# Gathered rows of a product-key layer: weights for two groups at once, two running sums, a ring of 24 rows

## The reference

```python
q = (hidden_states @ w_queries.T).reshape(b, t, 2, h, n)
sim = jnp.einsum('btphn,hkpn->pbthk', q, keys)
sx, ix = jax.lax.top_k(sim[0], k)
sy, iy = jax.lax.top_k(sim[1], k)
...
scores, pos = jax.lax.top_k(all_scores, k)
indices = jnp.take_along_axis(all_idx, pos, axis=-1)
de = down_embed[indices]
ue = up_embed[indices]
ew = jnp.einsum('btd,bthkd->bthk', hidden_states, de)
ew = jax.nn.silu(ew) * jax.nn.softmax(scores, axis=-1)
experts_states = jnp.einsum('bthk,bthkd->btd', ew, ue)
mlp = jax.nn.silu(hidden_states @ w_gate.T) * (hidden_states @ w_up.T) @ w_down.T
return mlp + experts_states
```

## Time and profile before

| | |
|---|---|
| median of 3 runs | 1626.28 us (1619.02 to 1626.79) |
| the profiled execution | 1626.24 us, of which its span is 1624.4 us |
| PE, DVE, ACT, POOL busy | 1293.6, 1102.0, 813.5, 699.8 us |
| mean granted TensorE clock | 0.872 of full speed |
| first gather starts, last gather starts | 308.9 us, 1157.2 us |
| last addition of layer 1 to x starts | 1170.0 us |

### The profile page before, as it was taken

How to read it: one execution, slowest core, us unless ns; L and a number is a source line. 1 busy time by engine, 2 the same in 40 slices (tenths; PEclk the granted TensorE clock), 3 DMA queues, 4 the chain that set the end, 5 groups by cost and what they waited for, 6 DMA issues and landing times.

```text
span 1624.4 us, 18804 instructions
## 1 busy us (share of the span) xinstructions
PE 1293.6 (80%) x5862; PEld 656.6 (40%) x5862; DVE 1102.0 (68%) x2921; ACT 813.5 (50%) x2053; POOL 699.8 (43%) x705
## 2 busy tenths in 40 slices
PE   5989886766678869477658676877889999999998
PEld 3345443243244525333323442443444455444444
DVE  6542417679996786898899998898864234336455
ACT  2454542656757768547558558657735432130110
POOL 2000000388888888854878778888500010010000
PEclk8899998877789979678768787989989999988999
DMA  6000000365575656743656765655310031002000
GB/s 229 23 1 1 10 6 2 63 180 162 164 172 170 187 164 194 183 122 93 179 157 173 223 173 177 182 165 164 110 24 1 1 124 34 1 28 72 1 14 26
DMA packets 59956, 168.67 MB, mean 104 GB/s; under 512 B 15760, under 2 KB 20944, under 8 KB 59216
## 3 DMA queue, kind: packets, MB, share of 16 engines
q0 software_dynamic: 40960, 134.25, 29.9%
q1 hardware_dynamic: 18896, 33.22, 6.3%
HBM read 162.61 MB, written 4.82 MB: 103 GB/s over the span
## 4 chain that ended last, share of the span: by engine, by line
PE 44%; DVE 22%; POOL 18%; issue 10%; ACT 3%; DMA 3%; SPq 0%; DVEq 0%; POOLq 0%; another core or an unknown queue 0%; ACTq 0%
POOL bufR L1851 15%; PE psum L1189 7%; PE psum L1051 6%; PE psum L1063 3%; DVE bufB L1547 3%; DVE bufR L1419 3%; POOL half_sum L1865 2%; PE psum L1108 2%; PE psum L1133 2%; PE psum L854 2%; DMA bufR<-in_table,rowid 2%; PE psum L933 2%; PE psum L986 2%; PE psum L816 2%; DVE x_sb L1437 2%
## 5 line engine op out<-in xcount | busy, mean ns | idle before, releaser
L1851 POOL DMA_INDIRECT bufR<-in_table,rowid x512 | 563.1, 1100 | 240.9 <-issue 124.8
L1214 ACT ACTIVATE bufR<-bufR 128x256 f32<-128x256 f32 x512 | 205.5, 405 | 49.0 <-DVE bufR L1419 37.7
L1419 DVE TENSOR_TENSOR bufR<-bufR 128x1024 f32<-128x1024 f32 x128 | 158.9, 1244 | 48.7 <-DMA bufR<-in_table,rowid 48.0
L854 PE MATMUL psum<-bufB 32*128 32x308 f32 x768 | 95.1, 572 | 93.9 <-DVE bufB L1547 64.7
L1051 PE MATMUL psum<-xtf,wf 128*128 128x512 f32 x320 | 156.3, 634 | 10.3 <-DVE x_sb L1704 7.5
L1547 DVE TENSOR_REDUCE bufB<-psum 128x8 f32<-128x1232 f32 x96 | 137.5, 1436 | 37.1 <-PE psum L854 32.6
L1223 ACT ACTIVATE bufR<-bufR,ew 128x256 f32<-128x256 f32 x128 | 64.0, 504 | 126.0 <-DVE ew L1427 80.9
L1482 DVE TENSOR_TENSOR x_sb<-x_sb,psum 128x256 f32<-128x256 f32 x128 | 50.6, 417 | 106.7 <-PE psum L986 58.6
L1878 POOL TENSOR_TENSOR x_sb<-x_sb,wattn 128x256 f32<-128x256 f32 x16 | 11.1, 730 | 253.9 <-DMA wattn<-in_attn 150.7
L1871 POOL TENSOR_TENSOR x_sb<-x_sb,wattn 128x256 f32<-128x256 f32 x32 | 23.7, 772 | 219.5 <-DMA wattn<-in_attn 161.5
L1811 DVE SCALAR_TENSOR_TENSOR x_sb<-psum,bufR,x_sb 128x256 f32<-128x256 f32 x128 | 61.9, 484 | 75.5 <-PE psum L1189 70.7
(11 more groups left out here) (237 smaller groups left out, 2504.0 us busy)
## 6 DMA issues: line engine op xcount, KB each, us to landing
bufR<-in_table,rowid POOLq DMA_INDIRECT x512
wf<-in_ffn SPq DMA_DIRECT2D x2, 2304.0 KB, 18.6
bufR<-in_ffn SPq DMA_DIRECT2D x1, 2696.5 KB, 17.2
wattn<-in_attn SPq DMA_DIRECT2D x4, 641.0 KB
wf<-in_rope SPq DMA_DIRECT2D x4, 512.0 KB
bufB<-in_ffn SPq DMA_DIRECT2D x1, 2048.0 KB, 8.3
scr_corr<-bufR SPq DMA_DIRECT2D x16, 128.0 KB, 2.3
bufR<-scr_corr SPq DMA_DIRECT2D x4, 512.0 KB, 4.6
```

The lines of the kernel that those rows point to most:

```text
L854: ins = mm(psum[:, at + z, 0:PAR * S], q[r, g, i * P:(i + 1) * P], keysm[r, g, b, :, 0:S], start=True, stop=True)
L1214: own.mark(act(row, row, ACT.Identity, accum_out=dots[:, g % 4, j:j + 1]))
L1419: tt(rows, rows, cast(xg[c % 2][:, i, :].unsqueeze(1), [P, GRP, D]), ALU.mult).then_inc(f1_mu, 1)
L1851: eng.indirect_dma_start(ring[:, s * GRP + j, :], None, io["table"], bass.IndirectOffsetOnAxis(ap=rowid[c % 2][:, at + j:at + j + 1], axis ...
```

## The change

- **Pairs.** The sums of two groups (2h and 2h+1) go to one row of eight. The tanh is taken once for both, behind the odd group, and `weights_of` makes eight weights at once. Weights, additions and the rows' scaling of the even group therefore wait for the odd group's rows.
- **Two sums.** `add_rows` adds rows 0 and 2 to x and row 1 to a tile `second`; only the third instruction waits, for the first. The first group of a tile writes `second` with a multiplication, so it waits for the tile before to be closed (`f1_tile`). `add_half` adds first `second` and then `half_sum` to x.
- **Plan.** `plan()` has the new dependences, new durations for `ew`, `ad` and `ga`, and another set of offsets `PREFER`, so the order of pieces on every engine may differ.

```diff
-RING, GRP = 20, 4
+RING, GRP = 24, 4
...
-             ew=0.41, ad=1.6, ga=0.42, Q=5.6, lg2=5.0, ...
+             ew=0.45, ad=1.5, ga=0.95, Q=5.6, lg2=5.0, ...
...
 PREFER = dict(
-    PE={("Q", 2): -200, ("gu2", 1, 6): -20, ("gu2", 3): 50, ("p1", 1): -160, ...
+    PE={("V3",): 315, ("gu2",): -10, ("gu2", 0): -40, ("p1",): 105, ("s", 2): -40, ...
...
+    POOL={("bo",): 160},
 )
...
-            a = add("ACT", ("th", g), 2.5, m, g >= 4 and ("DVE", ("ew", g - 4)))
-            e = add("DVE", ("ew", g), 0.45, a, g >= 4 and ("ACT", ("sc", g - 4)), g >= 4 and ("DVE", ("ad", g - 4)))
-            s = add("ACT", ("sc", g), 0.5, e)
-            add("DVE", ("ad", g), 1.65, e, outs[i], g and ("DVE", ("ad", g - 1)))
-            p = add("POOL", ("ad", g), 0.8, s, g and ("POOL", ("ad", g - 1)), first and g and ("DVE", ("ga", g - 1)))
+            a = add("ACT", ("th", g), 2.5, m, g >= 4 and ("DVE", ("ew", g // 2 - 2)))
+            if g % 2:
+                e = add("DVE", ("ew", g // 2), 0.45, a, g >= 4 and ("ACT", ("sc", g - 4)), g >= 4 and ("DVE", ("ad", g - 4)))
+                for n in (g - 1, g):
+                    s = add("ACT", ("sc", n), 0.5, e)
+                    add("DVE", ("ad", n), 1.5, e, outs[i], n and ("DVE", ("ad", n - 1)), n % NG == 0 and n and ("DVE", ("ga", n - 1)))
+                    p = add("POOL", ("ad", n), 0.8, s, n and ("POOL", ("ad", n - 1)), n % NG == 0 and n and ("DVE", ("ga", n - 1)))
...
+        def weight(g, j):
+            at = g % 2 * GRP + j
+            return ew[:, g // 2 % 2, at:at + 1]
...
-                own.wait()
-                act(thalf[:, g % 4, :], dots[:, g % 4, :], ACT.Tanh, scale=0.5).then_inc(f1_th, 1)
+                if g % 2:
+                    own.wait()
+                    h = g // 2 % 2
+                    act(thalf[:, h, :], dots[:, h, :], ACT.Tanh, scale=0.5).then_inc(f1_th, 1)
...
-            def weights_of(g):
-                c, s, at = g // UNITS, g % 4, g % UNITS * GRP
-                eng.wait_ge(f1_th, g + 1)
...
+            def weights_of(h):
+                c, z, at = 2 * h // UNITS, h % 2, 2 * h % UNITS * GRP
+                eng.wait_ge(f1_th, h + 1)
+                if h >= 2:
+                    eng.wait_ge(f1_wt, 2 * h - 2)
+                    eng.wait_ge(f1_acc, 2 * h - 2)
+                own.link(stt(ew[:, z, :], dots[:, z, :], 0.5, prob[c % 2][:, at:at + 2 * GRP], ALU.mult, ALU.mult))
+                stt(ew[:, z, :], thalf[:, z, :], 1.0, ew[:, z, :], ALU.add, ALU.mult).then_inc(f1_ew, 1)
...
-                own.link(stt(x, ring[:, at, D:2 * D], ew[:, g % 4, 0:1], x, ALU.mult, ALU.add))
-                own.link(stt(x, ring[:, at + 1, D:2 * D], ew[:, g % 4, 1:2], x, ALU.mult, ALU.add))
-                stt(x, ring[:, at + 2, D:2 * D], ew[:, g % 4, 2:3], x, ALU.mult, ALU.add).then_inc(f1_acc, 1)
+                own.mark(stt(x, rows[0], weight(g, 0), x, ALU.mult, ALU.add))
+                first = own.n
+                if g % NG == 0:
+                    own.mark(ts(second[:, :], rows[1], weight(g, 1), None, ALU.mult))
+                else:
+                    own.mark(stt(second[:, :], rows[1], weight(g, 1), second[:, :], ALU.mult, ALU.add))
+                eng.wait_ge(own_dve, first)
+                stt(x, rows[2], weight(g, 2), x, ALU.mult, ALU.add).then_inc(f1_acc, 1)
...
-                eng.wait_ge(f1_half, g + 1)
-                eng.wait_ge(f1_acc, g + 1)
+                eng.wait_ge(f1_acc, g + 1)
+                own.wait()
+                own.mark(tt(x, x, second[:, :], ALU.add))
+                eng.wait_ge(f1_half, g + 1)
+                own.wait()
                 tt(x, x, half_sum[:, :], ALU.add).then_inc(f1_tile, 1)
...
-    nc = _bacc.Bacc("TRN2", target_bir_lowering=False, num_devices=1)
+    nc = _bacc.Bacc("TRN2", target_bir_lowering=False, num_devices=1, dynamic_dma_scratch_size=4096)
```

More of the change, by code:

```diff
@@ L260, in ffn1 @@
         for g in range(UNITS * c, UNITS * (c + 1)):
-            first, back, last = g % NG == 0, g - SLOTS, g % NG == NG - 1
+            back, last = g - SLOTS, g % NG == NG - 1
             i = g // NG % TI
@@ L265, in ffn1 @@
             m = add("DVE", ("mu", g), 1.3, f, g and ("DVE", ("mu", g - 1)))
[L266 to L270 removed]
+            a = add("ACT", ("th", g), 2.5, m, g >= 4 and ("DVE", ("ew", g // 2 - 2)))
[5 more added lines that the diff above has]
+                    p = add("POOL", ("ad", n), 0.8, s, n and ("POOL", ("ad", n - 1)), n % NG == 0 and n and ("DVE", ("ga", n - 1)))
             if last:
[L272 removed]
+                add("DVE", ("ga", g), 0.95, p, ("DVE", ("ad", g)))
         return out, t
@@ L517, in build @@
         gate2 = sb("gate2", [P, KT * E2])
-        half_sum = sb("half_sum", [P, D])
+        half_sum, second = (sb(s, [P, D]) for s in ("half_sum", "second"))
         prob = [sb(f"prob{z}", [P, P]) for z in range(2)]
@@ L524, in build @@
         work1 = sb("work1", [P, 288])
-        dots, thalf, ew = (sb(s, [P, 4, GRP]) for s in ("dots", "thalf", "ew"))
+        dots, thalf, ew = (sb(s, [P, 2, 2 * GRP]) for s in ("dots", "thalf", "ew"))
         psum = ctx.enter_context(nc.psum_tensor("psum", [P, 8, 512], FP))
@@ L1210, in gathered_sums @@
                 if g >= 4:
-                    eng.wait_ge(f1_ew, g - 3)
+                    eng.wait_ge(f1_ew, g // 2 - 1)
                 for j in range(GRP):
                     row = ring[:, at + j, 0:D]
-                    own.mark(act(row, row, ACT.Identity, accum_out=dots[:, g % 4, j:j + 1]))
-                own.wait()
-                act(thalf[:, g % 4, :], dots[:, g % 4, :], ACT.Tanh, scale=0.5).then_inc(f1_th, 1)
-            def weighted_rows(g):
-                at = GRP * (g % SLOTS)
-                eng.wait_ge(f1_ew, g + 1)
-                for j in (3,):
-                    row = ring[:, at + j, D:2 * D]
-                    ins = act(row, row, ACT.Copy, scale=ew[:, g % 4, j:j + 1])
-                ins.then_inc(f1_wt, 1)
+                    own.mark(act(row, row, ACT.Identity, accum_out=dots[:, g // 2 % 2, g % 2 * GRP + j:g % 2 * GRP + j + 1]))
+                if g % 2:
+                    own.wait()
+                    h = g // 2 % 2
+                    act(thalf[:, h, :], dots[:, h, :], ACT.Tanh, scale=0.5).then_inc(f1_th, 1)
+            def weighted_rows(g):
+                row = ring[:, GRP * (g % SLOTS) + 3, D:2 * D]
+                eng.wait_ge(f1_ew, g // 2 + 1)
+                act(row, row, ACT.Copy, scale=weight(g, 3)).then_inc(f1_wt, 1)
             def deviation(tgt, layer, c):
@@ L1429, in add_rows @@
             def add_rows(g):
                 x, at = x_sb[:, g // NG, :], GRP * (g % SLOTS)
-                eng.wait_ge(f1_ew, g + 1)
+                rows = [ring[:, at + j, D:2 * D] for j in range(3)]
+                eng.wait_ge(f1_ew, g // 2 + 1)
                 if g % NG == 0:
                     eng.wait_ge(f1_x, g // NG + 1)
+                    if g:
+                        eng.wait_ge(f1_tile, g // NG)
                 if g:
                     eng.wait_ge(f1_acc, g)
-                own.link(stt(x, ring[:, at, D:2 * D], ew[:, g % 4, 0:1], x, ALU.mult, ALU.add))
```

19 lines of the change are left out of this document (7 added, 12 removed).

## The result

The changed kernel takes 1628.8 us (median of 20 runs, 1621.88 to 1633.01), the kernel before 1617.45 us (20 runs, 1614.18 to 1628.31). The ratio is 1.0056, 95% interval 1.004 to 1.0071: slower by 9 us (the medians lie 11 us apart), where 23 us less were forecast. The base of the forecast was off as well: the median of the three runs shown before (1626.28) and the profiled execution (1626.24) lie in the upper part of what 20 runs gave, 9 us above their median. So 1603 against 1628.8 shows 26 us of a miss of 32. The profiled execution of the changed kernel took 1629.35 us, its span is 1627.3 us.

A forecast was written before the change was run, and what follows sets the result against it. The prediction took POOL and DVE as near their limit in the gather phase, PE nearly the limit in the tail. Terms of -19, -9 and +5 us gave -23 us, from 1626.24 to 1603 us; range 1573 to 1636.

The forecast's parts named there:

- DVE's sum: DVE's work in the gather phase: additions 29 us and weights 17 us saved, closing tiles 8 us lost, 38 us less.
- The smaller space: Gathers on POOL: the smaller descriptor space was taken to cost nothing.
- the nothing of the sum: Closing a tile on DVE: the wait for `second` was taken as already done, at no cost.
- rival 3: Tile boundaries stall DVE, 2.8 us at each of 16, likewise some pairs' tanh waits: slower, 1657 us; chance 13%.
- From 38 us of DVE to time: Gather phase: DVE's saving becomes -19 us at the gap, -9 us in layer 2's steps, 5 us lost: -23 us.
- The gap, -19 us: POOL's 29.7 us of gaps ahead of chunk 2: the first half's DVE saving shortens them by 19 us.
- The steps of layer 2, -9 us: Second half of the gathers: layer 2's feed-forward steps go ahead, taking 9 us of PE work off the tail.
- The pairs, nothing in the sum: Ring slots and pair waits: the sixth group's slot offsets the even half's wait; 13.3 us of slot waits stay.
- The two sums, 21 us of DVE: DVE's additions to two sums: two links saved for each group, 29 us, less 8 us for closing tiles.
- What I drew from the rule: POOL's gathers and additions beside DVE: with as many two-input DVE instructions, the 85 us of POOL delay stay.
- (1), POOL holds the phase: Gather phase: DVE's time comes free where POOL doesn't wait, the 29.7 us gap stays: 1622 us; chance 16%.

The follow-up runs named there:

- e1: Kernel before with only the descriptor space cut to 4096 bytes a partition; median 1618.9 us.
- e9: Kernel before with small descriptor space and two sums, old order, the kernel of e2 again on another chip; ratio 1.0069 to the kernel before.
- e17: Kernel before with 24 rows, small descriptor space, pairs, one sum, old order, POOL's additions apart, e13 again on another chip; ratio 1.0213.
- e5: Kernel before with 24 rows, small descriptor space, pairs, one sum, old order, POOL's two additions of a pair together; ratio 1.0139.
- e3: Kernel before with small descriptor space and a ring of 24 rows, pieces in the old order; ratio 0.998 to the kernel before.
- e2: Kernel before with small descriptor space and two sums, two tiles `second` in turn, old order; ratio 1.0049 to the kernel before.
- e7: e2 with every addition linked to the one before it; ratio 1.0018 to the kernel before.
- e10: e9 with every addition linked to the one before it, on the same chip; ratio 1.0016 to the kernel before.
- e11: Changed kernel with all three additions of a group linked; ratio 1.0069 to the kernel before, median 1628.95 us.
- e4: All code of the change with pieces in the old order, POOL's two additions of a pair together; ratio 1.0086 to the kernel before.
- e16: Kernel before with 24 rows, small descriptor space, old order, fourth row of odd groups added on DVE instead of ACT and POOL; ratio 1.0324.
- e18: Kernel before with small descriptor space, POOL's copy and addition of the fourth row on 16 of 256 columns; ratio 0.9708, 1570.9 us.
- e15: The kernel of e18 on another chip; ratio 1.0205 to the kernel before, 1663.8 us.
- e8: Kernel before with small descriptor space, old order, row 1 of each group left out of the sum; ratio 0.9893, median 1620.0 us.
- e13: e5 with POOL's additions left where they were, apart; ratio 1.0173 to the kernel before.
- e6: The kernel of e18 on another chip, run earlier; ratio 1.0295 to the kernel before.
- e14: e4 with POOL's additions left where they were, apart; ratio 1.018 to the kernel before.

## Why the prediction was wrong

**What was right.** DVE's sum: 38 us forecast, 41.5 measured (47.1 less in the two stretches of the gathers, 5.1 more behind them). The additions stand as worked out, 0.40 us apart, and the third doesn't wait:

```profile
398.25 0.47 DVE L1451 SCALAR_TENSOR_TENSOR second<-bufR,ew,second 128x256 f32<-128x256 f32 x1
398.64 0.47 DVE L1453 SCALAR_TENSOR_TENSOR x_sb<-bufR,ew,x_sb 128x256 f32<-128x256 f32 x1
399.04 0.15 DVE L1433 SCALAR_TENSOR_TENSOR ew<-dots,prob 128x8 f32<-128x8 f32 x1
```

The gathers start where they did (308.2 us). The smaller space is free as far as e1 shows. POOL's gathers and additions stay as long as they were in the profile before (564.5 and 93.0 us against 563.1 and 90.7). The tile's close waits 18.0 us in 8 of 16 cases: more than the nothing of the sum, less than half of the 45 us that rival 3 had for it.

**The step that failed** is "From 38 us of DVE to time": the terms of -19 us and -9 us, and the pairs' term of nothing. It took POOL's work as a constant with a gap in it, and DVE's time as something that fills the gap. But from 309 to 700 us POOL has hardly an idle stretch over 0.55 us, one in either kernel (0.6 and 0.9 us), so what sets the end there is POOL's own row of instructions. Less work for DVE doesn't shorten that row, and the pairs and the new order put waits into it:

- *The gap, -19 us.* It gave 8, and 6.6 against e1. With 41 us less for DVE the row numbers of chunk 2 came 1 us earlier than in e1, counted from the first gather (432.9 against 434.0), and then the ring held the gather for another 1.2 us. That DVE is busy for 42.7 of the 45 us there is right; that its saved time comes off the gap isn't, and e9, where the wait is as long as in e1, says the same without pairs and new order.
- *The steps of layer 2, -9 us.* None came forward. L1058 (L1051 of the earlier trace rows) by stretch has 120 matmuls in place of 128 up to 1170, and up to its own last addition, which starts at 1174.9, the same 16 steps as before. The part behind the gathers is 465.7 us against 466.3:

```profile
954.00:1170.00 216.00, 68.41 (x120) 26.57 (x120) 0.89 0.57 161
1170.00:1300.00 130.00, 42.08 (x88) 16.85 (x88) 0.96 0.05 11
```

- *The pairs, nothing in the sum* ("the even half has what it had", "I let them stand"). Counted over all groups of the two traces, from a group's first gather to its last addition on DVE lie 24.8 us in the median before and 30.7 after; to POOL's addition 31.8 and 38.5. That is 5.9 and 6.6 us more, where the sixth slot gave 5.6. In the old order pairs and 24 rows cost 34 us (e17), or 23 where POOL's additions stand together (e5, on a chip with stalls). In e17 the even groups live 31.5 us up to DVE's addition and the odd ones 25.7, against 24.9 and 23.4 in e3: the even half doesn't have what it had. The new order pays in another place, with waits for slots, 23.5 us in place of 13.3 (18.8 of them in the gap ahead of chunk 2 that was just counted), and 5.0 of the copy behind the tile's close.
- *The two sums, 21 us of DVE.* They cost 8 to 11 us of time (e2, e9) in the old order, and nothing clear of noise with their links put back (1.0018 and 1.0016 in e7 and e10, both intervals take in 1). The rule of the Trainium skill (SBUF — State Buffer, "SBUF: two separate sides"), that a DVE instruction with two SBUF inputs and a GpSimd instruction that reads SBUF lock each other out for a whole instruction, fits the longer gathers in kind alone. In e1 a gather takes 0.97 us beside neither, 1.00 (142) beside additions alone, 1.24 (101) beside a multiplication alone and 1.315 (84) beside both, so the additions, which have two inputs too, hold it up little by themselves, and the trace agrees with the rule no further than that. What I drew from the rule, that an equal number of instructions gives an equal delay, isn't borne out either: e9 and e10 have the same instructions and differ by 7.9 us of gathers in their profiles and by 7.2 us of time. In the changed kernel's first chunk POOL has no long idle stretch at all, and from its first gather to the next chunk's lie 208.7 us in place of 201.1, with 143.6 us of gathers in place of 137.2. With linked additions (e11) these are 202.5 and 139.2, but chunk 3 is as slow as without links, 210.0 us.

Of the rivals, (1), POOL holds the phase, named the mechanism; its 1622 us, 4 less than its base, still had a gain where 9 us were lost. That 1622 looks near to 1628.8 is luck of the base, and so is that 1628.8 lies in the range of 1573 to 1636 (its lower end is 1574 by its own terms). With the base at 1617.45 the same range would end at 1627.

**What stays open.** The parts don't add up: two sums +8 to +11 and pairs with 24 rows +23 to +34 make more than the +14 of e4, and linking the additions helps without pairs (e10) and not with them (e11). Which part of the new order's remaining 9 us is due to which no run tells. How the loss divides between longer gathers and waits rests on one profile of each kernel. Whether work moved from POOL to DVE (e16) pays on a chip without stalls wasn't measured again.

## What to carry to other kernels

When two engines are near their limit in one phase, add up each one's own timeline, gaps and all, before work taken from the other is turned into time; here 41 us less for DVE gave nothing, and 55 less for POOL, with 44 less for DVE that followed from it, gave 47. A batch of two that saves 0.27 us of instructions lengthens the life of what it batches by up to a whole unit (5.6 us), and a ring, and every engine that takes the result in a fixed order, pays for it. Of the whole change at most the ring of 24 rows with the smaller space is worth keeping (0.998, 0.996 to 1.000); no other complete kernel here was faster.

## What the runs showed of the hardware that was not expected

**The same program, 93 us apart on two chips.** The kernel with short POOL additions took 1570.9 us (e18) and 1663.8 us (e15), where the kernel before differed by 11 us (1618.1, 1629.2). In the profile of e15 DVE and ACT stand idle for events whose source the profile can't name ("remote"), 86.5 and 70.2 us between 309 and 1200 us. Two such waits, the chain's shares, and one of the places (PE and ACT):

```profile
DVE x_sb L1482 <- remote: 49.8, 13, 13.3
ACT bufR L1296 <- remote: 18.9, 4, 7.3
```

```profile
PE 49%; DVE 23%; issue 9%; ACT 9%; another core or an unknown queue 5%; POOL 3%; DMA 2%; SPq 0%; DVEq 0%; ACTq 0%; POOLq 0%
```

```profile
792.23 1.07 PE L906 MATMUL psum<-bufR,bufB 128*32 128x512 f32 x8
...
794.29 1.06 PE L906 MATMUL psum<-bufR,bufB 128*32 128x512 f32 x8
...
799.24 0.31 PE L916 MATMUL psum<-const,bufR 128*128 128x128 f32 x1 [1.09 <-issue]
802.12 0.60 ACT L1296 ACTIVATE bufR<-psum 128x512 f32<-128x512 f32 x1 [7.28 <-remote]
807.08 0.60 ACT L1296 ACTIVATE bufR<-psum 128x512 f32<-128x512 f32 x1 [4.36 <-remote]
807.73 1.97 PE L916 MATMUL psum<-const,bufR 128*128 128x128 f32 x8 [8.17 <-issue]
```

Each of the two ACT instructions waits for one of the two blocks of L906. By the records these were done at 793.30 and 795.35, and ACT gets them 8.8 and 11.7 us later. PE then has no matmul for 8.2 us. The view names nothing that it waits for, but by the kernel's text the next transposes (L916) need the second ACT instruction, and they start 0.06 us after its end: PE's gap follows from ACT's delay. All eight profiles from the chips of e5 to e8 and e13 to e16 have such stalls (9.7 to 99.8 us an engine), the other ten of the experiments and that of the changed kernel have none (that of the kernel before 5.8 us on ACT and 3.6 on DVE). The least are in e8, the most in e6, e15 and e16, which leave POOL the least to do. What they are isn't known: PE's work finished later than its records say, or the event came late. Nor is it shown that they make up the whole difference between the chips. A verdict from one chip of this kind would have been the wrong way round: 1.0205 and 1.0295 where another chip gave 0.9708.

**An addition on POOL is cheap between two gathers and dear behind another addition**, by 0.24 us a pair: the short gaps of e4 and e5 are 15 us longer than those of e14 and e13, with 64 pairs.
